# One core, sparse attention and a routed FFN: the output projection's weights loaded in four steps and split head by head, and batch 0's fourth row block in another bank

## The chip, the cores and the metric

One core of a Trainium2 chip runs the whole kernel. The metric is device time in microseconds of one launch, the median of several runs.

## What is computed

The reference, cut to what matters (x is 8 x 512 x 512, H = 16 heads of HD = 128; `attn` mixes compressed, selected and windowed attention with three gates):

```python
z = layernorm(x)
q, k, v = rope(z @ Wq), rope(z @ Wk), z @ Wv      # per head: 512 x 128
o = o_cmp * g_cmp + o_slc * g_slc + o_swa * g_swa # per head and batch
x = x + concat_heads(o) @ Wo                      # Wo: 2048 x 512
x = x + routed_ffn(layernorm(x))                  # top 128 tokens of each batch, capacity 0.125
```

The change touches the place where the first two parts meet: the last heads of the attention, and `concat_heads(o) @ Wo` for batch 0.

## The kernel before, in words

Every product is made of three float32r matmuls, hi*hi, hi*lo and lo*hi, where hi is a rounded copy of an operand and lo is what rounding left out. So each operand needs a "high" (a copy, mostly on ScalarE) and a "low" (a subtraction on GpSimd or VectorE) before TensorE can use it.

**Attention** (`attend`, from line 425) runs over 128 *units*: 8 pairs of heads p, and in each 16 units, numbered u = 16p + 4k + j with k and j from 0 to 3. A unit is one head (s = j % 2) of one batch (b = 2k + j // 2). Every engine has its own program over units, and the order of the work is written out by hand in each; semaphores that count up join them. The stages of a unit are spread over three turns of the loop: in the body of u, TensorE projects q and k of u (L641), scores u - 1 (L684), transposes the probabilities of u - 2 (L698), projects the values of u (L654) and multiplies values with probabilities for u - 2 (L721). ScalarE's body (L804) begins with `output_out` (L783), the copy of a finished output to s_swap, then evacuates q, mixes the far blocks of u - 2 (L793), takes the high part of the values of u - 1 (L801), evacuates k, takes the high parts of the transposed probabilities (`pt_high`, L768), and does the exponentials (L774, L780) and the high parts of q and k (L763). VectorE's body (L928) masks and reduces the scores, takes `pt_low` (L894), forms the coefficients, mixes (L902, L918; the mix of blocks 2 and 1 waits for ScalarE's far mix) and ends with the values' low part (L924). GpSimd (L601) applies the rotary factors and takes the low parts of q and k. SyncE (L520) issues the store of an output (L508) and two swaps (L497, L498: the two halves of a rotated vector exchanged through a DMA), q's first and then k's, which also waits for the store. Unit "128" and "129" are bodies that finish the last two units and project nothing (`body(PAIRS, 0, ...)`).

**The end of attention.** The outputs of all units lie in DRAM. `Chunks` (from line 1050) multiplies them with Wo in four *chunks* of four heads for each batch, k = 0 to 3; `product` (L1103) does the 12 matmuls of each of four row blocks of a chunk into one PSUM bank per row block (`bank`, L1065: banks 4, 5, 7 and 3 for batch 0), which collects over the four chunks. Chunks alternate between two buffers. A chunk's semaphore `chunk_used` rises after its last row block. For batch 0 this is laid into attention's last units by hand:

- SP (L541 to L584): behind the first body of `quad(PAIRS - 1, 2)`, unit 120, all four Wo transfers; behind unit 124 the loads of chunks 0 and 1; the loads of chunks 2 and 3 behind the stores of bodies 129 and 130.
- ScalarE (L844 to L872): `high_wo`, two heads at a time, behind each of units 120 to 127; `high_first(0)`, the high part of chunk 0, behind unit 124; `high_first(1)` after unit 127; `high_first(2)` after body 129 and `high_first(3)` after the last output copy.
- GpSimd (L612 to L634): `low_wo` for heads 0 to 7 behind units 120 to 123, the two halves of chunk 0's low behind units 125 and 126, then chunks 1 to 3.
- VectorE (L988 to L1013): `low_wo` for heads 8 to 15 behind units 124 to 127.
- TensorE (L738 to L748):

```python
        chunks.product(pe, 0, 0, rows=(0,))
        pe.wait_ge(v_lo_done, U)
        body(PAIRS, 0, 0, project=False)
        chunks.product(pe, 0, 0, rows=(1, 2))
        chunks.product(pe, 0, 1, rows=(0, 1, 2))
        body(PAIRS, 0, 1, project=False, score=False, between=lambda: chunks.product(pe, 0, 0, rows=(3,)))
        chunks.product(pe, 0, 1, rows=(3,))
        for k in range(2, chunks.K):
            chunks.product(pe, 0, k)
```

The split buffers of Wo and of the chunks lie in the memory of the transposed inputs, xt_hi and xt_lo, which is why each load waits for a projection of the batch that it overwrites (`projected[2]`).

Of the kernel before, what the change touches and what calls it, by code (L numbers as in the profile page):

```python
# [7 lines left out]
H, HD = 16, 128  # L8
# [388 lines left out]
def attend(nc, phase, banks, m, gates, gates_full, xt_hi, xt_lo, weights, rope_d, misc_d, o_dram, gates_dram, chunks):  # L397
# [95 lines left out]
    def sync(sp):  # L493
# [46 lines left out]

        def quad(p, k, first=False, ahead=False, split=False, wo=False, o=False):  # L541
            body(p, k, 0, gate=first)
            if wo:
                sp.wait_ge(projected[2], unit(p, k, 0))
                for n in range(chunks.K):
                    chunks.load_wo(sp, n)
# [36 lines left out]
        chunks.load_first(sp, 3)  # L583
        sp.wait_ge(out_slot_free, 16 + 16 * U)  # L584

    def gpsimd(pool):
        def turn(u, k):

            pool.wait_ge(evacuated[k], u + 1)
            pool.wait_ge(swapped[k], u * 32 + 32)  # L590
            nc.gpsimd.tensor_tensor(s_full[k][:], s_full[k][:], rope[:, 0, :], ALU.mult).then_inc(cos_done[k], 1)  # L591
            nc.gpsimd.tensor_tensor(s_swap[k][:], s_swap[k][:], rope[:, 1, :], ALU.mult).then_inc(sin_done[k], 1)  # L592
            pool.wait_ge(cos_done[k], u + 1)
            pool.wait_ge(sin_done[k], u + 1)
# [17 lines left out]
        def quad(p, k, split=False, wo=False, o=False):  # L612
# [12 lines left out]
        pool.wait_ge(rope_loaded, 16)  # L625
        for k in range(0, 3):
            quad(0, k)
        for p in range(1, PAIRS):
            quad(p - 1, 3, split=p)
            for k in range(0, 3):  # L630
                quad(p, k, wo=p == PAIRS - 1 and k == 2)
        quad(PAIRS - 1, 3, o=True)
        for k in range(1, chunks.K):
            chunks.low(pool, 0, k)  # L634

    def tensor(pe):
# [21 lines left out]

        def body(p, k, j, project=True, score=True, end=True, between=None):
            u = unit(p, k, j)  # L660
# [41 lines left out]
            if project:  # L702
# [3 lines left out]
                project_values(b, s)  # L706
            if between is not None:
                between()
            if end:
# [4 lines left out]
                for i in range(T):  # L714
# [5 lines left out]
                    for v, x in ((v_hi, pt_hi), (v_hi, pt_lo), (v_lo, pt_hi)):  # L720
                        last = nc.tensor.matmul(banks[6][:, PTQ0[i]:N], v[:, slot, i % 2, :], x[:, PTOFF[i]:PTOFF[i] + w],  # L721
                                                start=(n == 0), stop=(n == 3 * T - 1), skip_group_check=True)
                        n += 1
# [19 lines left out]
        chunks.product(pe, 0, 0, rows=(1, 2))  # L743
        chunks.product(pe, 0, 1, rows=(0, 1, 2))
        body(PAIRS, 0, 1, project=False, score=False, between=lambda: chunks.product(pe, 0, 0, rows=(3,)))
        chunks.product(pe, 0, 1, rows=(3,))
        for k in range(2, chunks.K):
            chunks.product(pe, 0, k)  # L748

    def scalar(act):  # L750
# [32 lines left out]
        def output_out(u):  # L783

            act.wait_ge(out_ready, u - 2)
            act.wait_ge(out_slot_free, (u - 3) * 16 + 16)
            nc.scalar.activation(o_sb[:], banks[6][:, :], ACT.Copy).then_inc(out_evacuated, 1)

# [14 lines left out]

        def body(p, k, j, project=True, score=True, end=True, values=True, output=True, split=False):  # L804
            u = unit(p, k, j)
# [37 lines left out]

        def quad(p, k, split=False, wo=False, o=False):  # L844
# [18 lines left out]
        for p in range(1, PAIRS):  # L863
            quad(p - 1, 3, split=p)
            for k in range(0, 3):
                quad(p, k, wo=0 if p == PAIRS - 1 and k == 2 else False)
        quad(PAIRS - 1, 3, wo=4, o=True)
        body(PAIRS, 0, 0, project=False)
        body(PAIRS, 0, 1, project=False, score=False, values=False)
        chunks.high_first(act, 2)  # L870
        output_out(U + 2)
        chunks.high_first(act, 3)  # L872

    def vector(dve):
# [112 lines left out]

        def quad(p, k, split=False, wo=False):  # L988
            for j in range(4):
                body(p, k, j, split=split if j >= 2 else False)  # L990
                if wo:
                    chunks.low_wo(dve, nc.vector, 4 + j)

# [18 lines left out]
        quad(PAIRS - 1, 3, wo=True)  # L1012
        body(PAIRS, 0, 0, project=False)  # L1013
        body(PAIRS, 0, 1, project=False, score=False)

# [9 lines left out]
class Chunks:  # L1025
# [6 lines left out]
    def __init__(self, nc, at, banks, wo, o_dram):  # L1032
# [28 lines left out]
        self.hi_split, self.lo_split, self.chunk_used = S("hi_split"), S("lo_split"), S("chunk_used")  # L1061
        self.wo_hi_split, self.wo_lo_split = S("wo_hi_split"), S("wo_lo_split")
# [14 lines left out]
    def high_wo(self, act, n):  # L1077
        act.wait_ge(self.wo_loaded[n // 2], 16)
        self.nc.scalar.activation(self.wo_hi[:, 2 * n:2 * n + 2, :], self.wo_raw[:, 2 * n:2 * n + 2, :], ACT.Copy).then_inc(self.wo_hi_split, 1)

    def low_wo(self, eng, ops, n):
        eng.wait_ge(self.wo_hi_split, n + 1)
        ops.tensor_tensor(self.wo_lo[:, 2 * n:2 * n + 2, :], self.wo_raw[:, 2 * n:2 * n + 2, :],
                          f32(self.wo_hi[:, 2 * n:2 * n + 2, :]), ALU.subtract).then_inc(self.wo_lo_split, 1)

# [5 lines left out]

    def low_half(self, pool, k, g, last):
        pool.wait_ge(self.hi_split, k + 1)
        ins = self.nc.gpsimd.tensor_tensor(self.o_lo[k][:, g:g + 2], self.o_raw[k][:, g:g + 2], f32(self.o_hi[k][:, g:g + 2]), ALU.subtract)
        if last:
# [7 lines left out]
    def product(self, pe, b, k, rows=range(T)):  # L1103

        begun = isinstance(b, int) and b == 0
        if rows[0] == 0:
            pe.wait_ge(self.lo_split, b * self.K + k + 1)
            if begun:
                pe.wait_ge(self.wo_lo_split, 2 * k + 2)
        for t in rows:  # L1110
# [648 lines left out]
```

## Time and profile before

| | |
|---|---|
| median of 3 runs | 2390.52 us (2385.95 to 2391.7) |
| the profiled execution, its own time | 2390.49 us |
| its span, first to last instruction | 2388.7 us |
| mean granted TensorE clock | 0.992 |
| TensorE busy | 2313.6 us, 97% |
| VectorE, ScalarE, GpSimd busy | 77%, 62%, 68% |
| the chain that ended last | TensorE 67%, VectorE 11%, GpSimd 9%, ScalarE 5%, DMA 3% |

The span holds, in order, a normalisation of the inputs, attention up to about 1830 us, and the projection, routing and experts after it. The profile names an instruction by the line of the kernel that issues it; a helper's line stands for all its callers, so `L1083` is every low part of Wo. In a timeline a row is start, duration, engine, line, operation and operands, and in square brackets how long the engine was idle before and what released it.

### The profile page before, as it was taken

The page shows a single profiled execution, that of the slowest core. Times are in us where ns is not written, and L with a number is a line of the kernel's source. Part 1 is how long each engine was busy: PE and PEld are TensorE (multiplying, and loading weights), DVE is VectorE, ACT ScalarE, POOL GpSimd, SP SyncE. Part 2 cuts the span into 40 slices and gives each one's busy share as a digit, 9 for nine tenths or more (in the row PEclk, how much of TensorE's full clock was granted, in tenths as well). Part 3 has the DMA queues.
Part 4 walks back from the last instruction along what each step waited for, and adds up shares of the span by engine and source line. Part 5 has one row for each costly group of instructions (what it writes and reads, how often), then busy time and mean ns, then how long its engine had stood idle before and what let it go on. Part 6 is the DMA issues. An engine that isn't in the chain of part 4 may idle for free.

```text
span 2388.7 us, 42080 instructions
## 1 busy us (share of the span) xinstructions
PE 2313.6 (97%) x13200; PEld 2034.8 (85%) x13200; DVE 1836.8 (77%) x6087; ACT 1489.5 (62%) x4165; POOL 1632.8 (68%) x1267
## 2 busy tenths in 40 slices
PE   6999999999999999999999999999998999998998
PEld 5799899989888898999899898989887788886787
DVE  8589898988888898989898888888883665566311
ACT  6577777777777777777777777777773111212343
POOL 2677877787787778777877877787883444444554
PEclk9999999999999999999999999999999999999999
DMA  5222222222222223223222322222333444453332
GB/s 172 74 59 62 73 76 58 72 73 67 54 80 69 61 60 84 65 58 81 67 65 58 87 59 67 63 72 60 124 89 123 162 170 154 152 197 102 109 116 79
DMA packets 143602, 213.34 MB, mean 89 GB/s; under 512 B 15009, under 2 KB 53281, under 8 KB 143393
## 3 DMA queue, kind: packets, MB, share of 16 engines
q1 hardware_dynamic: 137248, 196.17, 27.8%
q10 hardware_dynamic: 4224, 8.39, 0.9%
q0 software_dynamic: 1920, 6.24, 0.8%
q8 instruction: 101, 1.65, 0.3%
q14 instruction: 109, 0.88, 0.1%
HBM read 90.47 MB, written 53.22 MB: 60 GB/s over the span
## 4 chain that ended last, share of the span: by engine, by line
PE 67%; DVE 11%; POOL 9%; ACT 5%; DMA 3%; issue 2%; SPq 0%; POOLq 0%; ACTq 0%; DVEq 0%
PE bank L641 19%; PE bank L1116 13%; PE bank L654 10%; PE bank L684 7%; PE bank L721 7%; PE bank L698 4%; DMA s_swap<-s_full 3%; PE bank L1677 3%; PE bank L1658 3%; POOL s_full L591 2%; POOL s_swap L592 2%; POOL s_full L595 2%; DVE bank L884 1%; DVE shift L880 1%; DVE pt_lo L894 1%
## 5 line engine op out<-in xcount | busy, mean ns | idle before, releaser
L591 POOL TENSOR_TENSOR s_full<-s_full,rope 128x512 f32<-128x512 f32 x256 | 336.5, 1314 | 334.9 <-DMA s_swap<-s_full 334.5
L595 POOL TENSOR_TENSOR s_full<-s_full,s_swap 128x512 f32<-128x512 f32 x256 | 330.7, 1292 | 37.6 <-POOL s_swap L592 0.9
L592 POOL TENSOR_TENSOR s_swap<-s_swap,rope 128x512 f32<-128x512 f32 x256 | 330.7, 1292 | 0.0
L599 POOL TENSOR_TENSOR qk_lo<-s_full,qk_hi 128x512 fp32r<-128x512 f32 x256 | 326.2, 1294 | 0.1
L768 ACT ACTIVATE pt_hi<-bank 128x384 fp32r<-128x384 f32 (+1 forms) x384 | 174.5, 528 | 229.1 <-PE bank L698 229.0
L654 PE MATMUL bank<-wv_hi,xt_hi 128*128 128x256 f32 x1024 | 300.1, 293 | 0.0
L774 ACT ACTIVATE bank<-bank,shift 128x512 f32<-128x512 f32 (+3 forms) x512 | 256.9, 502 | 60.1 <-DVE bank L884 59.8
L1100 POOL TENSOR_TENSOR o_lo<-o_raw,o_hi 128x2048 fp32r<-128x2048 f32 x31 | 142.3, 4591 | 217.6 <-ACT o_hi L1276 185.9
L654 PE MATMUL bank<-wv_hi,xt_lo 128*128 128x256 f32 x1024 | 289.7, 283 | 0.0
L654 PE MATMUL bank<-wv_lo,xt_hi 128*128 128x256 f32 x1024 | 289.7, 283 | 0.0
L884 DVE TENSOR_REDUCE bank<-bank 128x8 f32<-128x512 f32 (+3 forms) x512 | 253.1, 494 | 0.0
L880 DVE TENSOR_REDUCE shift<-bank 128x1 f32<-128x512 f32 (+3 forms) x512 | 246.3, 481 | 0.0
L902 DVE SCALAR_TENSOR_TENSOR bank<-bank,coef,cb 128x192 f32<-128x192 f32 (+1 forms) x512 | 195.5, 405 | 58.6 <-ACT probs L793 58.6
L780 ACT ACTIVATE win<-win,shift 128x192 f32<-128x192 f32 (+1 forms) x512 | 225.8, 441 | 0.0
L763 ACT ACTIVATE qk_hi<-s_full 128x512 fp32r<-128x512 f32 x256 | 161.4, 630 | 93.1 <-POOL s_full L595 89.1
L894 DVE TENSOR_TENSOR pt_lo<-bank,pt_hi 128x384 fp32r<-128x384 f32 (+1 forms) x384 | 206.9, 594 | 8.7 <-ACT pt_hi L768 8.7
L641 PE MATMUL bank<-xt_hi,wq_hi 128*128 128x512 f32 x512 | 207.8, 406 | 0.8 <-PEq L201 0.8
L1116 PE MATMUL bank<-wo_hi,o_hi 128*128 128x512 f32 x512 | 205.9, 402 | 2.1 <-POOL o_lo L1100 2.1
L1116 PE MATMUL bank<-wo_hi,o_lo 128*128 128x512 f32 x512 | 200.6, 392 | 0.0
L641 PE MATMUL bank<-xt_hi,wq_lo 128*128 128x512 f32 x512 | 200.4, 391 | 0.0
L1116 PE MATMUL bank<-wo_lo,o_hi 128*128 128x512 f32 x512 | 200.1, 391 | 0.0
L641 PE MATMUL bank<-xt_hi,wk_lo 128*128 128x512 f32 x512 | 199.2, 389 | 0.0
(189 smaller groups left out, 6899.0 us busy)
## 6 DMA issues: line engine op xcount, KB each, us to landing
s_swap<-s_full SPq DMA_DIRECT2D x512, 128.0 KB, 2.3
o_scratch<-s_swap SPq DMA_DIRECT2D x128, 256.0 KB, 2.0
o_raw<-o_scratch SPq DMA_DIRECT2D x32, 1024.0 KB, 5.4
w_raw<-in_L_ffn_W SPq DMA_DIRECT2D x64, 256.0 KB, 2.9
xin<-in_L_attn_x SPq DMA_DIRECT2D x14, 1024.0 KB, 5.6
z_scratch<-z ACTq DMA_DIRECT2D x8, 1024.0 KB, 4.3
out<-x SPq DMA_DIRECT2D x32, 256.0 KB, 2.1
wq_raw<-in_L_attn_Wq SPq DMA_DIRECT2D x16, 256.0 KB, 3.1
```

Of the source, the lines that this page charges most:

```text
L591: nc.gpsimd.tensor_tensor(s_full[k][:], s_full[k][:], rope[:, 0, :], ALU.mult).then_inc(cos_done[k], 1)
L592: nc.gpsimd.tensor_tensor(s_swap[k][:], s_swap[k][:], rope[:, 1, :], ALU.mult).then_inc(sin_done[k], 1)
L595: nc.gpsimd.tensor_tensor(s_full[k][:], s_full[k][:], s_swap[k][:], ALU.add).then_inc(roped[k], 1)
L599: nc.gpsimd.tensor_tensor(qk_lo[k][:], s_full[k][:], f32(qk_hi[k][:]), ALU.subtract).then_inc(lo_done[k], 1)
L641: last = nc.tensor.matmul(banks[QK_BANK[k]][:, :], w[k][s][:, c, :], v[:, b, c, :], start=(n == 0), stop=(n == 3 * C - 1))
L654: last = nc.tensor.matmul(out, x[:, b, c, at:at + P], w[:, c, :], start=(n == 0), stop=(n == 3 * C - 1), skip_group_check=True)
L774: nc.scalar.activation(n, n, ACT.Exp, bias=shift1[:, t:t + 1], scale=-1.0, accum_out=sums[:, 1, t:t + 1]).then_inc(exp_row, 1)
L780: nc.scalar.activation(win[:, t, lo:], win[:, t, lo:], ACT.Exp, bias=shift2[:, t:t + 1], scale=-1.0, accum_out=sums[:, 2, t:t + 1]).then_i ...
L880: nc.vector.tensor_reduce(shift1[:, t:t + 1], n[:, 0:(t + 1) * P], AX.X, ALU.min)
L884: nc.vector.reduce_sum(sc[:, t, 0:nb], n[:, 0:nb * BS].rearrange("p (n s) -> p n s", s=BS), AX.X).then_inc(row_read, 1)
L894: nc.vector.tensor_tensor(pt_lo[:, PTOFF[g]:PTOFF[g] + w], pt_bank(u, g)[:, 0:w], f32(pt_hi[:, PTOFF[g]:PTOFF[g] + w]), ALU.subtract).then ...
L1116: last = self.nc.tensor.matmul(self.bank(b, t)[:, :], o[k % 2][:, g, t * P:(t + 1) * P], w[:, k * self.G + g, :], start=(k == 0 and n == 0 ...
```

## The change

Wo's transfers are issued one by one, behind units 114, 116, 118 and 120. Wo's high and low parts are made per head (128 x 512) and no longer per two heads: high parts of heads 0 to 9 behind units 116 to 123, 126 and 127, those of 10 to 15 after body 128; low parts of heads 0 to 7 on GpSimd behind units 117 to 124, those of 8 to 15 on VectorE after body 128. Chunk 0's high part is made in two halves behind units 124 and 125, and its low part in four operations; chunk 1's load is issued behind unit 126, its high part made inside body 128 after the values' high part; chunk 2's high part is made inside body 129. The loads of chunks 2 and 3 each move up by one store. Batch 0's fourth row block collects in bank 6, which held the outputs of units; the output of body 129 goes to bank 0 and its transposes to banks 0, 1 and 2. TensorE does row block 3 of chunk 0 and all of chunk 1 before body 129.

```diff
-            return banks[((6, 5, 7), (6, 0, 1))[u - U][g]]
+            return banks[((6, 5, 7), (0, 1, 2))[u - U][g]]
+    def out_bank(u):
+        return banks[0 if isinstance(u, int) and u == U + 1 else 6]
...
+        def load_wo(p, k, j, n):
+            sp.wait_ge(projected[2], unit(p, k, j))
+            chunks.load_wo(sp, n)
+
+        def quad(p, k, first=False, ahead=False, split=False, wo=(), o=False):
             body(p, k, 0, gate=first)
+            if 0 in wo:
+                load_wo(p, k, 0, wo[0])
             if o:
                 sp.wait_ge(projected[2], unit(p, k, 0))
                 chunks.load_first(sp, 0)
-                chunks.load_first(sp, 1)
             body(p, k, 1, ahead=ahead)
             body(p, k, 2, split=split)
+            if 2 in wo:
+                load_wo(p, k, 2, wo[2])
+            if o:
+                chunks.load_first(sp, 1)
             body(p, k, 3, split=split)
...
-        quad(PAIRS - 1, 0, first=True)
-        quad(PAIRS - 1, 1)
-        quad(PAIRS - 1, 2, wo=True)
+        quad(PAIRS - 1, 0, first=True, wo={2: 0})
+        quad(PAIRS - 1, 1, wo={0: 1, 2: 2})
+        quad(PAIRS - 1, 2, wo={0: 3})
         quad(PAIRS - 1, 3, o=True)
         body(PAIRS, 0, 0, project=False, gate=True)
+        chunks.load_first(sp, 2)
         body(PAIRS, 0, 1, project=False)
-        chunks.load_first(sp, 2)
+        chunks.load_first(sp, 3)
         body(PAIRS, 0, 2, project=False)
-        chunks.load_first(sp, 3)
...
@@ gpsimd: quad, and its calls @@
-                if wo:
-                    chunks.low_wo(pool, nc.gpsimd, j)
+                if j in wo:
+                    chunks.low_wo(pool, nc.gpsimd, wo[j], chunks.wo_lo_split)
                 if o and j in (1, 2):
-                    chunks.low_half(pool, 0, 2 * (j - 1), j == 2)
+                    chunks.low_half(pool, 2 * (j - 1), j == 2)
-                quad(p, k, wo=p == PAIRS - 1 and k == 2)
-        quad(PAIRS - 1, 3, o=True)
+                quad(p, k, wo=({}, {1: 0, 2: 1, 3: 2}, {0: 3, 1: 4, 2: 5, 3: 6})[k] if p == PAIRS - 1 else {})
+        quad(PAIRS - 1, 3, wo={0: 7}, o=True)
...
@@ tensor @@
         body(PAIRS, 0, 0, project=False)
         chunks.product(pe, 0, 0, rows=(1, 2))
-        chunks.product(pe, 0, 1, rows=(0, 1, 2))
-        body(PAIRS, 0, 1, project=False, score=False, between=lambda: chunks.product(pe, 0, 0, rows=(3,)))
-        chunks.product(pe, 0, 1, rows=(3,))
+        pe.wait_ge(out_evacuated, U)
+        chunks.product(pe, 0, 0, rows=(3,))
+        chunks.product(pe, 0, 1)
+        body(PAIRS, 0, 1, project=False, score=False)
...
@@ scalar: body (behind values_high and evacuate(u, 1)), quad, and its calls @@
+            if first is not False:
+                chunks.high_first(act, first)
...
-                if wo is not False:
-                    chunks.high_wo(act, wo + j)
-                if o and j == 0:
-                    chunks.high_first(act, 0)
-            if o:
-                act.wait_ge(projected[2], U)
-                chunks.high_first(act, 1)
+                if j in wo:
+                    chunks.high_wo(act, wo[j])
+                if o and j < 2:
+                    chunks.high_half(act, 2 * j)
...
-                quad(p, k, wo=0 if p == PAIRS - 1 and k == 2 else False)
-        quad(PAIRS - 1, 3, wo=4, o=True)
-        body(PAIRS, 0, 0, project=False)
-        body(PAIRS, 0, 1, project=False, score=False, values=False)
-        chunks.high_first(act, 2)
+                quad(p, k, wo=({}, {0: 0, 1: 1, 2: 2, 3: 3}, {0: 4, 1: 5, 2: 6, 3: 7})[k] if p == PAIRS - 1 else {})
+        quad(PAIRS - 1, 3, wo={2: 8, 3: 9}, o=True)
+        body(PAIRS, 0, 0, project=False, first=1)
+        for n in range(10, H):
+            chunks.high_wo(act, n)
+        body(PAIRS, 0, 1, project=False, score=False, values=False, first=2)
         output_out(U + 2)
         chunks.high_first(act, 3)
...
@@ vector @@
-                if wo:
-                    chunks.low_wo(dve, nc.vector, 4 + j)
         body(PAIRS, 0, 0, project=False)
+        for n in range(8, H):
+            chunks.low_wo(dve, nc.vector, n, chunks.wo_late_split)
         body(PAIRS, 0, 1, project=False, score=False)
...
@@ Chunks @@
-        return self.banks[(4, 5, 7, 3)[t] if isinstance(b, int) and b == 0 else t]
+        return self.banks[(4, 5, 7, 6)[t] if isinstance(b, int) and b == 0 else t]
...
+    def high_half(self, act, g):
+        act.wait_ge(self.raw_loaded[0], 16)
+        self.nc.scalar.activation(self.o_hi[0][:, g:g + 2], self.o_raw[0][:, g:g + 2], ACT.Copy).then_inc(self.hi_split if g else self.first_hi_split, 1)
...
+                if k < 2:
+                    pe.wait_ge(self.wo_lo_split, self.G * (k + 1))
+                else:
+                    pe.wait_ge(self.wo_late_split, self.G * (k - 1))
```

## Rows read from the trace of the kernel before

**Rows 1.** The page: TensorE's busy time and share of the span.
```profile
PE 2313.6 (97%) x13200; PEld 2034.8 (85%) x13200; DVE 1836.8 (77%) x6087; ACT 1489.5 (62%) x4165; POOL 1632.8 (68%) x1267
```

**Rows 2.** Windows: length, busy of PE, PEld, DVE, ACT, POOL; clock, DMA.
```profile
1443.32:1549.79 106.47, 106.37 (x659) 96.18 (x658) 94.99 (x340) 78.32 (x239) 80.19 (x64) 1.00 0.24 65
1619.59:1672.85 53.26, 53.26 (x330) 48.05 (x330) 47.20 (x171) 38.44 (x118) 39.30 (x32) 1.00 0.23 60
1672.85:1788.21 115.36, 109.75 (x659) 97.02 (x658) 95.57 (x334) 85.68 (x248) 97.28 (x71) 0.99 0.36 110
1788.21:1830.92 42.71, 32.77 (x155) 27.46 (x154) 22.14 (x75) 19.26 (x52) 14.38 (x7) 0.92 0.19 62
```

**Rows 3.** Windows of single units on TensorE, 122 and 123.
```profile
1700.05:1716.23 16.18, 13.76 (x85) 11.88 (x84) 11.72 (x44) 12.03 (x35) 15.10 (x12) 1.00 0.19 50
1716.23:1729.76 13.53, 13.50 (x84) 11.93 (x84) 11.68 (x44) 10.60 (x32) 12.29 (x10) 1.00 0.23 60
```

**Rows 4.** The tile wo_raw: times in ns and starts; DMA landing.
```profile
L1083 POOL TENSOR_TENSOR wo_lo<-wo_raw,wo_hi x4: 2364/2388/2397, 1691.1 to 1734.5; 128x1024 fp32r<-128x1024 f32 x4
L1083 DVE TENSOR_TENSOR wo_lo<-wo_raw,wo_hi x4: 1215/1216/2362, 1752.8 to 1798.2; 128x1024 fp32r<-128x1024 f32 x4
DMA to landing us min/median/max: 6.0/9.1/11.3
```

**Rows 5.** Timeline of SP's queue, units 121, 124 and 125.
```profile
1691.24 0.47 SPq L497 DMA_DIRECT2D s_swap<-s_full  x1
...
1695.88 0.46 SPq L497 DMA_DIRECT2D s_swap<-s_full  x1
...
1738.01 1.19 SPq L1075 DMA_DIRECT2D o_raw<-o_scratch  x2
...
1750.03 0.47 SPq L497 DMA_DIRECT2D s_swap<-s_full  x1
...
1752.23 0.46 SPq L497 DMA_DIRECT2D s_swap<-s_full  x1
```

**Rows 6.** Timeline of VectorE: far-mix waits, a v_lo, a pt_lo.
```profile
1664.20 0.75 DVE L902 SCALAR_TENSOR_TENSOR bank<-bank,coef,cb 128x192 f32<-128x192 f32 x2 [0.24 <-ACT probs L793]
...
1665.51 0.68 DVE L924 TENSOR_TENSOR v_lo<-bank,v_hi 128x512 fp32r<-128x512 f32 x1
...
1721.85 0.75 DVE L902 SCALAR_TENSOR_TENSOR bank<-bank,coef,cb 128x192 f32<-128x192 f32 x2 [0.93 <-ACT probs L793]
...
1796.30 0.75 DVE L902 SCALAR_TENSOR_TENSOR bank<-bank,coef,cb 128x192 f32<-128x192 f32 x2 [2.24 <-ACT probs L793]
...
1821.48 1.62 DVE L894 TENSOR_TENSOR pt_lo<-bank,pt_hi 128x512 fp32r<-128x512 f32 x3 [7.57 <-ACT pt_hi L768]
```

**Rows 7.** Timeline of ScalarE at the end of attention.
```profile
1792.04 1.05 ACT L1079 ACTIVATE wo_hi<-wo_raw 128x1024 fp32r<-128x1024 f32 x1
1792.99 1.90 ACT L1090 ACTIVATE o_hi<-o_raw 128x2048 fp32r<-128x2048 f32 x1
...
1794.79 0.59 ACT L787 ACTIVATE s_swap<-bank 128x512 f32<-128x512 f32 x1
...
1810.08 0.59 ACT L787 ACTIVATE s_swap<-bank 128x512 f32<-128x512 f32 x1
```

**Rows 8.** Timeline of TensorE from unit 128 to chunk 2.
```profile
1798.34 0.48 PE L684 MATMUL bank<-qk_hi,qk_hi 128*128 128x128 f32 x1 [7.17 <-DVE v_lo L924]
...
1806.55 0.44 PE L1116 MATMUL bank<-wo_hi,o_hi 128*128 128x512 f32 x1
...
1820.22 1.25 PE L698 MATMUL bank<-misc,probs 128*128 128x128 f32 x10
...
1830.92 0.50 PE L1116 MATMUL bank<-wo_hi,o_hi 128*128 128x512 f32 x1 [2.06 <-POOL o_lo L1100]
```

**Rows 9.** A window in unit 128's scores, columns as in rows 2.
```profile
1800.00:1802.00 2.00, 2.00 (x8) 1.90 (x7) 1.90 (x7) 0.00 (x0) 0.00 (x0) 0.50 0.00 0
```

**Rows 10.** Timeline of GpSimd: the low part of chunk 1.
```profile
1794.97 4.52 POOL L1100 TENSOR_TENSOR o_lo<-o_raw,o_hi 128x2048 fp32r<-128x2048 f32 x1 [1.30 <-ACT o_hi L1090]
```

More of the change, by code:

```diff
@@ L539, in body @@
                 weights.load_v(sp, ahead)
-        def quad(p, k, first=False, ahead=False, split=False, wo=False, o=False):
+        def load_wo(p, k, j, n):
+            sp.wait_ge(projected[2], unit(p, k, j))
+            chunks.load_wo(sp, n)
+        def quad(p, k, first=False, ahead=False, split=False, wo=(), o=False):
             body(p, k, 0, gate=first)
-            if wo:
-                sp.wait_ge(projected[2], unit(p, k, 0))
-                for n in range(chunks.K):
-                    chunks.load_wo(sp, n)
+            if 0 in wo:
+                load_wo(p, k, 0, wo[0])
             if o:
@@ L610, in body, with quad @@
                 weights.low(pool, nc.gpsimd, split, 1, j % 2)
-        def quad(p, k, split=False, wo=False, o=False):
+        def quad(p, k, split=False, wo=(), o=False):
             for j in range(4):
                 body(p, k, j, split if j >= 2 else False)
-                if wo:
-                    chunks.low_wo(pool, nc.gpsimd, j)
+                if j in wo:
+                    chunks.low_wo(pool, nc.gpsimd, wo[j], chunks.wo_lo_split)
                 if o and j in (1, 2):
-                    chunks.low_half(pool, 0, 2 * (j - 1), j == 2)
+                    chunks.low_half(pool, 2 * (j - 1), j == 2)
         nc.gpsimd.memset(shift2[:], 0.0).then_inc(out_slot_free, 16)
@@ L657, in project_values, with body @@
             last.then_inc(projected[2], 1)
-        def body(p, k, j, project=True, score=True, end=True, between=None):
+        def body(p, k, j, project=True, score=True, end=True):
             u = unit(p, k, j)
@@ L706, in body @@
                 project_values(b, s)
-            if between is not None:
-                between()
             if end:
@@ L720, in body @@
                     for v, x in ((v_hi, pt_hi), (v_hi, pt_lo), (v_lo, pt_hi)):
-                        last = nc.tensor.matmul(banks[6][:, PTQ0[i]:N], v[:, slot, i % 2, :], x[:, PTOFF[i]:PTOFF[i] + w],
+                        last = nc.tensor.matmul(out_bank(u)[:, PTQ0[i]:N], v[:, slot, i % 2, :], x[:, PTOFF[i]:PTOFF[i] + w],
                                                 start=(n == 0), stop=(n == 3 * T - 1), skip_group_check=True)
@@ L786, in output_out @@
             act.wait_ge(out_slot_free, (u - 3) * 16 + 16)
-            nc.scalar.activation(o_sb[:], banks[6][:, :], ACT.Copy).then_inc(out_evacuated, 1)
+            nc.scalar.activation(o_sb[:], out_bank(u - 1)[:, :], ACT.Copy).then_inc(out_evacuated, 1)
         def mix_far(v, t):
@@ L802, in values_high, with body @@
                                  banks[7][:, :].rearrange("p (a n) -> p a n", a=2), ACT.Copy).then_inc(v_hi_done, 1)
-        def body(p, k, j, project=True, score=True, end=True, values=True, output=True, split=False):
+        def body(p, k, j, project=True, score=True, end=True, values=True, output=True, split=False, first=False):
             u = unit(p, k, j)
@@ L842, in body, with quad @@
                 weights.high(act, split, 1, j % 2)
-        def quad(p, k, split=False, wo=False, o=False):
+        def quad(p, k, split=False, wo=(), o=False):
             for j in range(4):
                 body(p, k, j, split=split if j >= 2 else False)
-                if wo is not False:
-                    chunks.high_wo(act, wo + j)
-                if o and j == 0:
-                    chunks.high_first(act, 0)
-            if o:
-                act.wait_ge(projected[2], U)
-                chunks.high_first(act, 1)
+                if j in wo:
+                    chunks.high_wo(act, wo[j])
+                if o and j < 2:
+                    chunks.high_half(act, 2 * j)
         nc.scalar.activation(gates_full[:], gates_full[:], ACT.Sigmoid).then_inc(gates_squashed, 1)
@@ L986, in body, with quad @@
                 weights.low(dve, nc.vector, split, 0, j % 2)
-        def quad(p, k, split=False, wo=False):
+        def quad(p, k, split=False):
             for j in range(4):
                 body(p, k, j, split=split if j >= 2 else False)
-                if wo:
-                    chunks.low_wo(dve, nc.vector, 4 + j)
         nc.vector.memset(sc, 0.0).then_inc(zeros_set, 3)
@@ L1077, in high_wo, with low_wo @@
     def high_wo(self, act, n):
-        act.wait_ge(self.wo_loaded[n // 2], 16)
-        self.nc.scalar.activation(self.wo_hi[:, 2 * n:2 * n + 2, :], self.wo_raw[:, 2 * n:2 * n + 2, :], ACT.Copy).then_inc(self.wo_hi_split, 1)
-    def low_wo(self, eng, ops, n):
+        act.wait_ge(self.wo_loaded[n // self.G], 16)
+        self.nc.scalar.activation(self.wo_hi[:, n, :], self.wo_raw[:, n, :], ACT.Copy).then_inc(self.wo_hi_split, 1)
+    def low_wo(self, eng, ops, n, split):
         eng.wait_ge(self.wo_hi_split, n + 1)
-        ops.tensor_tensor(self.wo_lo[:, 2 * n:2 * n + 2, :], self.wo_raw[:, 2 * n:2 * n + 2, :],
-                          f32(self.wo_hi[:, 2 * n:2 * n + 2, :]), ALU.subtract).then_inc(self.wo_lo_split, 1)
+        ops.tensor_tensor(self.wo_lo[:, n, :], self.wo_raw[:, n, :], f32(self.wo_hi[:, n, :]), ALU.subtract).then_inc(split, 1)
+    def high_half(self, act, g):
+        act.wait_ge(self.raw_loaded[0], 16)
+        self.nc.scalar.activation(self.o_hi[0][:, g:g + 2], self.o_raw[0][:, g:g + 2], ACT.Copy).then_inc(self.hi_split if g else self.first_hi_split, 1)
     def high_first(self, act, k):
@@ L1090, in high_first, with low_half @@
         self.nc.scalar.activation(self.o_hi[k % 2][:], self.o_raw[k % 2][:], ACT.Copy).then_inc(self.hi_split, 1)
-    def low_half(self, pool, k, g, last):
-        pool.wait_ge(self.hi_split, k + 1)
-        ins = self.nc.gpsimd.tensor_tensor(self.o_lo[k][:, g:g + 2], self.o_raw[k][:, g:g + 2], f32(self.o_hi[k][:, g:g + 2]), ALU.subtract)
+    def low_half(self, pool, g, last):
+        pool.wait_ge(self.hi_split if g else self.first_hi_split, 1)
+        for i in range(g, g + 2):
+            ins = self.nc.gpsimd.tensor_tensor(self.o_lo[0][:, i], self.o_raw[0][:, i], f32(self.o_hi[0][:, i]), ALU.subtract)
         if last:
```

6 lines of the change are left out of this document (3 added, 3 removed).

## The prediction

> **What bounds the kernel now.** I read the page first: TensorE (PE) is busy 97% of a span of 2388.7 us [rows 1]. A change can gain only where PE idles, runs at the lower clock, or is held to another engine's pace. So I read stretches of PE's work next [rows 2]. Undisturbed, eight units (one head of one batch each) take 106.47 us, 13.31 each. Units 116 to 119 take 53.26, the same pace. The last eight, 120 to 127, take 115.36: 8.9 us too long. From the last unit's end, 1788.21 (called S below), to the first product of chunk 2, 1830.92, pass 42.71 us with PE busy 32.77. Those two stretches are all that the diff touches.
>
> Inside the slow eight most units take about 13.53, as unit 123 does, and unit 122 takes 16.18 [rows 3]. Three causes can be read off. First, the four Wo transfers are issued together and take 6.0 to 11.3 us to land [rows 4]; the swap traffic behind them ran into them: unit 121's two swaps are issued 4.64 us apart, where 2.20 is usual (unit 125's) [rows 5]. Second, ScalarE (ACT) splits a Wo part between a unit's last high part and the output copy; behind that copy stand the far mixes that VectorE (DVE) waits for. That wait is 0.24 us without Wo work, 0.93 with it, and 2.24 in the last unit, where the split of chunk 1 stands there too [rows 6]. Third, DVE has its own Wo part, 1.22 us, in units 124 to 127 [rows 4].
>
> At the end PE does row 0 of chunk 0, then idles 7.17 us for the last v_lo, and starts unit 128 at 1798.34 = S+10.13. After it come five product rows, then unit 129 with one row on either side of its values, and a 2.06 us wait for chunk 2's low part [rows 8].
>
> **Units 116 to 127.** ACT's eight Wo splits of 128x1024 become sixteen of one head: ten in units 116 to 123, 126 and 127, six after unit 128. The 128x1024 one costs ACT 0.95 us from start to start, the 128x2048 one 1.80 [rows 7]; on that line one of 128x512 costs 0.52. Units 121 and 123 carried 0.95 of it and took 13.53; taking back 0.43 gives 13.1, under PE's own 13.31, so these units are PE's again. Units 124 and 125 carry half of chunk 0 each, 128x1024, as unit 123 carried a Wo part: 13.55.
>
> POOL's eight heads in units 117 to 124 cost half of 2.39 us each [rows 4], in its waiting for swaps: with a whole 2.39 it was busy 12.29 of unit 123's 13.53 us [rows 3]. The two halves of chunk 0's low (two operations each now, the same columns) lie there in units 125 and 126. If that cover went, each would delay the next unit's scores by up to 1.2 us.
>
> SP issues the four Wo transfers singly, behind the second swap of units 114, 116, 118 and 120, and chunk 1's load behind 126's. Each is some 10 us ahead of the next store; issuing one costs SP 0.5 us, with nothing due. The two 1 MB loads at 1738.01 stood in the same place, and the next pair of swaps left 2.20 us apart, 12 us later [rows 5]. So I take no cost; the bounds are 0 and 2.9 us a load, the excess of unit 122 behind the burst of four.
>
> Sum: ten units at 13.37 (13.31 and a little for the fuller ACT) and two at 13.55 are 160.8 us, against 53.26 + 115.36 = 168.6. Gain **7.8 us**. Bounds: 9.0 (all at 13.3) and 5.9 (all at 13.56).
>
> **From S to chunk 2.** Before the last v_lo ACT has one head (0.52) instead of a Wo part and chunk 1 (2.75 [rows 7]): 2.2 us less, and DVE's wait of 2.24 [rows 6] shrinks to little. DVE's own Wo work in the four units is gone as well, so it no longer lags PE. In a steady unit v_lo ended at 1666.19, 6.6 us after PE began that unit (1659.60, one steady 13.25 before unit 120). I take S+7.0, where it was S+10.1. Gain **3.1**, bounds 2.4 and 3.5. Next after it comes POOL's low part of k at S+5.5, not later.
>
> Unit 128 itself is 8.2 us up to 1806.55 (T) [rows 8]; about 2.5 of it is the granted clock of 0.50, the 1.2 GHz level, after the idle time [rows 9]. I keep that: PE still idles 4 us. Chunk 1's high split (1.8 us) moves inside this unit on ACT, ahead of pt_high; what hides it is PE's scores and transposes, 3.7 us or more. POOL's low of chunk 1 follows it and must be there for PE at T+10; it is 9 us early.
>
> The work from T to chunk 2 stays 22.3 us (24.37 less the wait of 2.06), but its order brings two waits. **Row 3 of chunk 0** now uses bank 6, so PE stands before it until ACT has copied out unit 128's output (out_evacuated of U). ACT reached that copy at 1810.08, T+3.5; now the six left-over heads are in front of it: 6 x 0.52 = 3.1, plus 0.59 for the copy: T+7.3. PE is through rows 1 and 2 after 24 products of 0.228 (60 of them took 13.67 [rows 8]), T+5.5. Cost **1.8**, bounds 1.5 and 2.5, and all of PE's queue stands behind it. **Unit 129** has no product row between its transposes and its values any more. DVE's first pt_lo began 1.26 after the transposes did [rows 6, 8] and lasts about 0.6; PE is done with them at +1.0. Cost **1.0**, bounds 0.7 and 1.5.
>
> The wait of 2.06 goes: chunk 2's split needs chunk 0 used, now near T+10, then 1.9 on ACT and 4.5 on POOL, and PE comes for it at T+25. Its load and chunk 3's move up by one store on SP; chunk 3's waits there for chunk 1's low, long done. Chunk 3 has the whole of chunk 2, 10.9 us, for its own 6.5.
>
> The eight heads that DVE splits after unit 128 start when the far mixes, behind ACT's six heads, are done: about T+10. Eight at half of 1.22 end at T+15; PE asks for DVE's next pt_lo near T+22. Nothing.
>
> POOL can take from that cover. The one DVE Wo part that began (1798.2) while POOL worked on chunk 1's low took 2.36 us, not 1.22 [rows 4], ending 1.07 after POOL's did [rows 10]: it waited for it. The same beside chunk 2's low, from T+12 to T+16.7, puts the eight heads at T+20: 2 us are left.
>
> The Trainium skill, page "SBUF — State Buffer", section "Who interferes with whom", says that GpSimd and a VectorE operation with two SBUF inputs lock each other out for a whole instruction. By that rule the trace agrees.
>
> **Sum.** 7.8 + 3.1 + 2.06 - 1.8 - 1.0 = 10.2 us. After chunk 2 each step waits for steps that moved along with it, so the gain stays. The profiled execution took 2390.49 us, 1.8 around its span; the median of three is 2390.52, so the sum holds for both: 2380.3. A measurement of this kernel can tell about 0.3%, 7.2 us, from no change.
>
> **Rivals.**
> 1. ACT sets the pace in all twelve units, 13.56 each: they give 5.9 and the total is 8.3 us, 2382.2. For it: DVE waits for ACT's far mixes even without Wo work, 0.24 us. Against: there it did not lengthen the unit. Chance 0.17.
> 2. The end is tighter than I count: the wait before row 3 drops the clock again, 1.5 us as a part of what it cost in unit 128, and the DVE heads are 2 us late for pt_lo, with a second hold by POOL. Then 10.2 - 3.5 = 6.7 or a little less: near 2384. Against: 2 us of slack, and 5.5 us of dense products before the wait. Chance 0.13.
> 3. Slower: each single Wo load delays the next store and swaps as the burst did, 2.9 us at four places, 11.6 in all; 10.2 becomes -1.4: 2391.9. It decides where a load still runs 10 us after its issue. The burst's first landed in 6.0 [rows 4], so one alone would have to be much slower than one of four. Chance 0.06.
> 4. It doesn't do what it says: the slow units owe their time to something that stays. Then only the end gains, 2 to 5 us: 2387. Against: the waits on ACT and the swaps name Wo work each time. Chance 0.07.
>
> The forecast has 0.57. Its own range, from the bounds (9.0 + 3.5 + 2.1 - 1.5 - 0.7 = 12.4; 6.5 + 2.4 + 2.1 - 2.5 - 1.5 = 7.0), is 2378 to 2383.5. The range of 8 in 10 takes in the second rival and something of the spread of the runs (2385.95 to 2391.7): 2375.5 to 2386.5. Faster by more than 0.3% (below 2383.3) holds the forecast, most of rival 1 and a third of rival 2: 0.74. Within 0.3%: 0.22. Slower: 0.04.
>
> **What would show it.** Units 121 to 127 of 13.3 to 13.6 us, none of 16; swaps never over 2.5 us apart; PE's idle time before unit 128 near 4 us; a new PE wait for ACT's copy before row 3 of chunk 0, 1.5 to 2; about 1 us before unit 129's values; none before chunk 2; 40.3 us from S to chunk 2. I am wrong if the twelve units take over 163 us, if POOL or a swap shows as PE's releaser in them, or if the time from S to chunk 2 is not under 42.7.

## The result and the profile after

The changed kernel takes 2376.74 us (median of 6 runs, 2373.81 to 2379.06) against 2390.72 for the kernel before; the ratio is 0.9939, 95% interval 0.9929 to 0.9949. That is 14 us less (12.2 to 17.0), where 10.2 were forecast. A second, separate set gave 0.9932 (0.9919 to 0.9945). The forecast's own range was 2378 to 2383.5 and its wide one 2375.5 to 2386.5: the measured time lies 1.3 us under the first and inside the second. One of the 12 executions of a kernel below, the one with the end's order alone, ran in a slow state (2985.89 us at a granted clock of 0.72) and is left out of its ratio.

The first view is that of rows 2 and 3: windows of the changed kernel's profiled execution (span 2377.1 us). In order: units 116 to 119, units 120 to 127, unit 122 alone, and the last unit's end to chunk 2. Columns as in rows 2.

```profile
1619.18:1672.99 53.81, 53.49 (x330) 48.00 (x330) 46.94 (x169) 39.07 (x120) 41.47 (x34) 1.00 0.35 99
1672.99:1781.31 108.32, 107.56 (x658) 95.76 (x658) 93.38 (x336) 83.50 (x252) 94.69 (x76) 1.00 0.30 88
1700.75:1714.02 13.27, 13.27 (x84) 12.00 (x84) 11.76 (x44) 10.33 (x33) 11.58 (x10) 1.00 0.23 61
1781.31:1820.69 39.38, 32.23 (x155) 26.71 (x154) 23.53 (x76) 20.49 (x55) 15.45 (x6) 0.96 0.21 68
```

Units 116 to 119 take half a microsecond more (53.26 before), units 120 to 127 give 7.0 (115.36), unit 122 alone 2.9 (16.18 [rows 3]), and the end gives 3.3 (42.71).

More than unit 122's 2.9 comes from a unit whose length neither the rows nor the forecast give. Unit 125 of the kernel before (first line) took 16.94 us, the longest of the eight, and takes 13.63 in the changed one (second line):

```profile
1743.49:1760.43 16.94, 15.10 (x84) 13.53 (x84) 13.29 (x48) 12.97 (x35) 11.66 (x9) 0.90 0.28 87
1740.54:1754.17 13.63, 13.51 (x85) 11.94 (x84) 11.38 (x42) 10.45 (x30) 11.50 (x10) 1.00 0.22 60
```

What it waited for before, on ScalarE, VectorE and TensorE:

```profile
1746.18 1.05 ACT L1079 ACTIVATE wo_hi<-wo_raw 128x1024 fp32r<-128x1024 f32 x1
1747.13 1.91 ACT L1090 ACTIVATE o_hi<-o_raw 128x2048 fp32r<-128x2048 f32 x1
1748.93 0.59 ACT L787 ACTIVATE s_swap<-bank 128x512 f32<-128x512 f32 x1
...
1750.92 0.75 DVE L902 SCALAR_TENSOR_TENSOR bank<-bank,coef,cb 128x192 f32<-128x192 f32 x2 [2.73 <-ACT probs L793]
...
1752.04 0.69 PE L684 MATMUL bank<-qk_hi,qk_hi 128*128 128x384 f32 x1 [1.84 <-DVE probs L918]
```

A Wo part and the whole high part of chunk 0 stood before ScalarE's output copy, 2.75 us, as chunk 1's did in the last unit. The change puts half a chunk there instead, and no Wo head: VectorE's wait is 1.33 us and TensorE's is gone.

Next SP's queue around unit 121, to set beside rows 5, and the landing of the Wo transfers from the tile's view.

```profile
1681.81 0.60 SPq L1079 DMA_DIRECT2D wo_raw<-in_L_attn_Wo  x1
1691.45 0.34 SPq L512 DMA_DIRECT2D o_scratch<-s_swap  x1
1691.94 0.47 SPq L501 DMA_DIRECT2D s_swap<-s_full  x1
...
1694.13 0.46 SPq L501 DMA_DIRECT2D s_swap<-s_full  x1
...
DMA to landing us min/median/max: 5.4/6.4/7.1
```

The last single Wo transfer leaves 9.6 us before the next store and has landed by then (7.1 us at most), and the two swaps of unit 121 are 2.19 us apart and no longer 4.64.

TensorE from the end of the units to chunk 2, as in rows 8:

```profile
1788.09 0.47 PE L693 MATMUL bank<-qk_hi,qk_hi 128*128 128x128 f32 x1 [3.81 <-DVE v_lo L932]
...
1793.67 0.47 PE L728 MATMUL bank<-pt_hi,v_hi 128*128 128x512 f32 x1 [0.85 <-ACT pt_hi L776]
...
1802.91 0.50 PE L1132 MATMUL bank<-wo_hi,o_hi 128*128 128x512 f32 x1 [1.63 <-ACT s_swap L795]
...
1818.75 0.47 PE L728 MATMUL bank<-pt_hi,v_hi 128*128 128x512 f32 x1 [0.85 <-ACT pt_hi L776]
```

The idle time before unit 128 has gone from 7.17 to 3.81 us and the 2.06 before chunk 2 are gone. Two waits are new: 1.63 for ScalarE's copy before row 3 of chunk 0, and 0.85 before unit 129's values.

### The profile page after: what moved, and what is told of

It is laid out like the page before. It is cut to its first block, busy times and chain, and to the rows that moved or that the text cites. A ratio compares the mean times of both kernels' runs of the same rounds, so it can differ in the third digit from the quotient of the medians.

```text
span 2377.1 us, 42098 instructions
## 1 busy us (share of the span) xinstructions
PE 2309.4 (97%) x13200; PEld 2031.2 (85%) x13200; DVE 1844.1 (78%) x6091; ACT 1489.1 (63%) x4174; POOL 1633.4 (69%) x1273
## 4 chain that ended last, share of the span: by engine, by line
PE 66%; DVE 11%; POOL 9%; ACT 5%; DMA 3%; issue 2%; SPq 0%; POOLq 0%; ACTq 0%; DVEq 0%
PE bank L650 19%; PE bank L1132 13%; PE bank L663 10%; PE bank L693 7%; PE bank L728 7%; PE bank L707 4%; DMA s_swap<-s_full 3%; PE bank L1693 3%; PE bank L1674 3%; POOL s_full L600 3%; POOL s_swap L601 3%; POOL s_full L604 3%; DVE bank L892 1%; DVE pt_lo L902 1%; DVE shift L888 1%
## 5 line engine op out<-in xcount | busy, mean ns | idle before, releaser
L650 PE MATMUL bank<-xt_hi,wk_hi 128*128 128x512 f32 x512 | 199.2, 389 | 0.0
```

Of the source, the lines that this page charges most:

```text
L650: last = nc.tensor.matmul(banks[QK_BANK[k]][:, :], w[k][s][:, c, :], v[:, b, c, :], start=(n == 0), stop=(n == 3 * C - 1))
```

## The experiments

**The end's order alone, and all but the end's order.** The first kernel is the one before with the change's banks and TensorE order; the second is the changed one with those of before:

```diff
...
-        chunks.product(pe, 0, 1, rows=(0, 1, 2))
-        body(PAIRS, 0, 1, project=False, score=False, between=lambda: chunks.product(pe, 0, 0, rows=(3,)))
-        chunks.product(pe, 0, 1, rows=(3,))
+        pe.wait_ge(out_evacuated, U)
+        chunks.product(pe, 0, 0, rows=(3,))
+        chunks.product(pe, 0, 1)
+        body(PAIRS, 0, 1, project=False, score=False)
...
```

> The kernel before with the end's order of the change alone: bank 6 for the fourth row block, TensorE's row 3 of chunk 0 and all of chunk 1 ahead of unit 129, the loads of chunks 2 and 3 one store earlier, chunk 2's high part inside body 129. The Wo work over the units stays. Theory A (the order itself gains little, its new waits eat the 2.06 us wait that goes): without the six heads in front of ScalarE's output copy no wait before row 3, about 0.9 us before unit 129's values, none before chunk 2: the time from unit 128's end to chunk 2 goes from 24.4 to 23.2 us, total -1.2 us (-0.05%). Theory B (the order is where the gain that I did not forecast lies): -4 us or more.

> The changed kernel with the end's order of before: banks 3 and 6 as before, five product rows and then unit 129, chunk 2's load and high part as before. Theory A (the gain is the Wo work over the units and the earlier v_lo): from 1619 to the last unit's end 162 us as in the changed kernel, 24.4 us from unit 128's end to chunk 2 instead of its 25.1, so the same as or 0.7 us under the changed kernel, -12 to -15 us against before. Theory B (the order carries it): only -8 to -10 us.

The order alone: 2389.53 us, ratio 0.9992 (0.9983 to 1.0000). From unit 128's end to chunk 2 it took 1830.37 - 1807.21 = 23.16 us, 1.2 less than before, as theory A had it. All but the order: 2374.88 us, ratio 0.9938 (0.9925 to 0.9950), not to be told from the changed kernel; by the medians it is 15.5 us under the kernel before, half a microsecond more than theory A's 12 to 15. Its units 116 to 127 took 160.22 us, and its old order ends in the old wait:

```profile
1817.21 0.50 PE L1134 MATMUL bank<-wo_hi,o_hi 128*128 128x512 f32 x1 [2.06 <-POOL o_lo L1115]
```

That is 24.40 us from unit 128's end (1792.81), against 25.10 in the changed kernel. With the six heads in front of the output copy the new order costs 0.7 us; only without them is it a gain.

**Only the Wo transfers, and only VectorE's Wo parts.** The first issues the four transfers singly as the change does. The second moves `low_wo` on VectorE:

```diff
-        quad(PAIRS - 1, 3, wo=True)
+        quad(PAIRS - 1, 3)
         body(PAIRS, 0, 0, project=False)
+        for n in range(4, 8):
+            chunks.low_wo(dve, nc.vector, n)
```

> The kernel before with the four Wo transfers issued singly behind units 114, 116, 118 and 120, all else unchanged. Theory A (the burst cost unit 122 its 2.9 us, and a single load costs nothing): unit 122 goes from 16.18 to about 13.5 us, no other unit longer, total -2.7 us (-0.11%). Rival (a single load costs as well, or unit 122 is long for another reason): 0 or slower, with late swaps in units 115, 117, 119 or 121.

> The kernel before with VectorE's four Wo parts (1.22 us each) moved behind its body of unit 128, all else unchanged. Theory A (they set the pace of units 125 to 127): those go from 13.3, 14.7 us and the lag before the last v_lo to 13.5 each, PE's idle time before unit 128 from 7.17 to about 5.5 us (ScalarE's 2.75 us before the copy stay), total -3 to -4 us. Rival (ScalarE's splits alone hold these units): under 1 us.

Single transfers: 2386.72 us, ratio 0.9989 (0.9980 to 0.9997). Unit 122 took 13.65 us, 2.5 less, units 115 to 119 13.26 each, unit 120 13.99: theory A. Unit 125 still took 16.92 us. (A slip stands at unit 120 in nearly every kernel, 13.3 to 14.3 us, with Wo loads near it or without.) VectorE's parts moved: 2387.5 us, ratio 0.9991 (0.9982 to 0.9999). From unit 123 to unit 128's scores it took 1796.20 - 1717.62 = 78.58 us, against 82.11 before and 81.45 in the second profile of the kernel before, below: 3.5 and 2.9 less, near theory A's 3 to 4, with 6.20 us of idle time left before unit 128. But units 125 to 127 took 15.43, 13.54 and 13.69 us, not 13.5 each. In unit 125 TensorE still waited, 1.90 us, so VectorE's part was not what held it there:

```profile
1744.38:1759.81 15.43, 13.53 (x84) 11.96 (x84) 11.72 (x44) 12.48 (x33) 10.25 (x9) 1.00 0.31 94
```

That unit took 16.9 to 17.1 us in four profiles, at a clock of 0.90, and 15.4 in two, at 1.00; TensorE's wait was 1.84 to 1.94 in all six. With the Wo transfers and VectorE's parts each ruled out by a run, ScalarE's 2.75 us remain, which the waits name; no run moved them alone.

One thing here I had not looked for. The kernel with VectorE's parts moved still has the burst, and its unit 122 took 19.11 us; that of the kernel with the order alone took 18.06.

**The same two kernels again.**

> The changed kernel as it is, for a second profile and a tighter ratio. Theory A (I sized the removed burst by one profile in which unit 122 took 16.18 us, while two others with the burst showed 18.06 and 19.11): units 121 to 124 within 13.3 to 13.6 us each again, 161 to 163 us for units 116 to 127, 39 to 40 us from the last unit's end to chunk 2, and -13 to -14 us against before. Rival (the extra gain lies in something of the changed kernel's that its first profile did not show): a stretch over 1 us shorter than in that profile.

> The kernel before as it is, for a second profile. Theory A (the burst of Wo transfers costs a varying amount, 2.9 us in the first profile and 4.8 and 5.9 in two other kernels that kept it): unit 122 between 16 and 19.5 us, the stall of 3.5 to 4 us at GpSimd's indirect DMA in the experts present again, PE's idle time before unit 128 7.17 us. Rival (18 and 19 us came from those kernels' own edits): unit 122 at 16.2 again.

The windows of the changed kernel again: units 116 to 127, then to chunk 2, then to the end. Behind them those of the kernel before again, with unit 122 third.

```profile
1618.73:1778.86 160.13, 159.86 (x987) 144.07 (x986) 140.76 (x504) 123.14 (x370) 136.10 (x109) 1.00 0.32 93
1778.86:1818.41 39.55, 32.33 (x154) 26.83 (x154) 23.52 (x76) 20.56 (x55) 15.51 (x6) 0.96 0.20 67
1818.41:2373.40 554.99, 532.18 (x2354) 433.87 (x2353) 267.65 (x567) 146.74 (x186) 253.60 (x150) 0.99 0.42 142
```

```profile
1619.44:1790.59 171.15, 163.97 (x986) 146.21 (x986) 143.18 (x502) 124.75 (x364) 136.77 (x102) 0.98 0.31 93
1790.59:1832.83 42.24, 32.18 (x155) 26.86 (x154) 22.11 (x75) 19.29 (x52) 14.32 (x7) 0.92 0.19 63
1699.65:1719.25 19.60, 16.45 (x85) 14.57 (x84) 13.13 (x50) 13.63 (x43) 18.21 (x15) 0.83 0.15 41
1832.83:2390.50 557.67, 533.26 (x2352) 434.74 (x2352) 259.40 (x565) 146.24 (x185) 253.00 (x150) 0.99 0.41 141
```

The burst's price varies, and the first profile had it at its cheapest: unit 122 took 16.18, 18.06, 19.11, 17.63 and 19.60 us in the five profiles that have the burst, 18.1 on the mean, so 4.8 over 13.3 instead of 2.9. The clock column (third from the right) goes with it: 1.00 in the first [rows 3], 0.91, 0.82, 0.90 and 0.83 in the others, so for a part of the unit the granted clock was at its lower level, 1.2 GHz. The length of the wait alone does not decide that: TensorE's wait for GpSimd's low part before the unit's scores was 1.64 us in the first and 2.66, 1.74, 1.71 and 2.35 in the others. Theory A for the changed kernel missed two numbers: its units took 160.1 us, below 161 to 163, and by the ratio it gained 16.3 us, above 13 to 14. By its wording the rival holds as well, since the units were 2.0 us shorter than in the first profile and the stretch after chunk 2 1.4. In the kernel before again, unit 122 was 0.1 above the forecast's 19.5.

**After chunk 2.** The last windows above show 2.7 us that the change gains where it touches nothing. The first pair of profiles has 557.8 and 556.4 us there. TensorE's rows with idle time differ by more than half a microsecond in one place, in the experts. GpSimd and TensorE in the kernel before:

```profile
2243.38 0.18 POOL L1583 CAST row_at<-away 128x1 int32<-128x1 f32 x1
2247.09 1.11 POOL L1588 DMA_INDIRECT rows<-out,row_at  x1 [3.53 <-issue]
```

```profile
2249.55 0.50 PE L1658 MATMUL bank<-zsel_hi,w_hi 128*128 128x512 f32 x1 [1.82 <-POOL w_lo L1576]
```

And GpSimd at the same place in the changed kernel:

```profile
2234.80 0.18 POOL L1599 CAST row_at<-away 128x1 int32<-128x1 f32 x1
2235.82 1.11 POOL L1604 DMA_INDIRECT rows<-out,row_at  x1 [0.84 <-POOL row_at L1599]
```

GpSimd stood 3.5 us with nothing to wait for ("issue"), the next weight's low part came late, and TensorE waited 1.82 us. So I made GpSimd's program six instructions longer, and nothing else:

```diff
-        nc.gpsimd.memset(mc[:], 0.0).then_inc(chunks.chunk_used, 1)
+        for t in range(T - 1):
+            nc.gpsimd.memset(mc[:, t:t + 1], 0.0)
+        nc.gpsimd.memset(mc[:, T - 1:T], 0.0).then_inc(chunks.chunk_used, 1)
...
```

> The kernel before with three memsets on GpSimd, at the start of attention, split into nine: the same values, six more instructions in GpSimd's program, as many as the change adds there, and no other edit. Theory A (in the experts, 420 us after attention, GpSimd stands 3.5 to 4.0 us at one indirect DMA with nothing to wait for, in all four kernels with the old GpSimd program and in none of the six with the longer one; the place of the instructions in memory decides): the stall at that DMA goes or moves, TensorE's wait of 1.8 to 2.3 us for w_lo behind it goes with it, total -1.8 us (-0.08%). Rival (the stall has to do with the Wo work or the end's order): it stays at 3.5 us or more at the same line, total 0.

2386.25 us, ratio 0.9983 (0.9974 to 0.9992), and the same DMA has its usual wait:

```profile
2243.25 1.11 POOL L1593 DMA_INDIRECT rows<-out,row_at  x1 [0.84 <-POOL row_at L1588]
```

The stall stood in all five profiles with the old GpSimd program and in none of the seven with a longer one, and six more memsets, 2170 us earlier, take it away.

The 4.1 us between the medians (1.9 to 6.2 by the interval) are more than the 1.8 that I expected, because the wait is not the whole price. The matmuls behind it, 2249.55 to 2254.23, ran at a granted clock of 0.64. From the matmul behind an earlier wait of 0.9 us to the span's end it took, before and with the longer program (columns as in rows 2):

```profile
2239.25:2388.70 149.45, 140.12 (x604) 113.99 (x604) 24.93 (x34) 60.50 (x99) 83.81 (x81) 0.97 0.35 108
2238.10:2384.60 146.50, 138.60 (x604) 112.86 (x604) 32.91 (x34) 60.39 (x98) 84.10 (x81) 0.99 0.35 110
```

It was 149.45 to 149.95 us in the five profiles with the stall and 146.42 to 146.52 in the seven without: the stall costs 3.3 us on the means. What lies between chunk 2 and there took 405.0 to 410.0 us in the twelve profiles, whether they have the stall or not, so the 2.7 and 1.4 us of the two pairs are the stall's price with this scatter on top.

That six instructions more in the program decide is shown, for this one length. That the stall is the loading of code is not, but the DMA view points there. In the window of the stall, 2243.56 to 2247.09, the queue marked "instruction" has one packet (count, MB, share):

```profile
q14 instruction: 1, 0.01, 0.7%
```

The same holds for the stall in each of the five profiles. In the seven others that queue has no packet in the 3.5 us before the same DMA. Whose instructions they are the profile doesn't say.

**Toward a better kernel.** Three edits to the changed one: ScalarE's six heads behind the output copy; TensorE's wait for the last v_lo moved to the first transposes that write its bank; a product row in front of unit 129's values.

```diff
-        for n in range(10, H):
-            chunks.high_wo(act, n)
-        body(PAIRS, 0, 1, project=False, score=False, values=False, first=2)
+        body(PAIRS, 0, 1, project=False, score=False, values=False, first=2, heads=range(10, H))
...
-        pe.wait_ge(v_lo_done, U)
         body(PAIRS, 0, 0, project=False)
...
+                    if not project and g == 2:
+                        pe.wait_ge(v_lo_done, U)
...
-        chunks.product(pe, 0, 1)
-        body(PAIRS, 0, 1, project=False, score=False)
+        chunks.product(pe, 0, 1, rows=(0, 1, 2))
+        body(PAIRS, 0, 1, project=False, score=False, between=lambda: chunks.product(pe, 0, 1, rows=(3,)))
```

> The changed kernel with ScalarE's six left-over Wo heads moved behind the output copy and the far mixes of body 129. Theory A (they alone are what TensorE waits for before row 3 of chunk 0): the wait of 1.63 us goes to 0, 0.85 before unit 129's values stays, from unit 128's end to chunk 2 23.5 us instead of 25.1; total -1.6 us against the changed kernel, so about -15.5 against before. Rival (the copy is late for the exponentials before it): a wait of over 0.5 us stays.

> The changed kernel with TensorE's wait for the last v_lo moved from before unit 128 to before its third group of transposes, the first that writes v_lo's bank. Theory A (the idle time before unit 128 is that wait, and next come the low parts of q and k, ready near S+4.7): scores start at S+4.7 instead of S+6.8, PE's idle time 3.8 us goes to about 1.7, and the granted clock stays at 1.00, so that the scores take 2.1 us and not 3.5: -2 to -3.4 us against the changed kernel. Rival (the scores wait for the mixed probabilities of unit 126 instead, which come from the same far mixes): -0.5 us or less.

> The changed kernel with both edits, and with row 3 of chunk 1 between unit 129's transposes and its values, to cover the 0.85 us there. Theory A: the three add up: no wait before row 3, none before unit 129's values, 22.6 us from unit 128's end to chunk 2, unit 128 2 to 3.4 us earlier; -4.5 to -6 us against the changed kernel, near 2371.5 us. Rival (each hides behind the other): -3 or less.

Copy first: 2373.69 us, ratio to before 0.9925 (0.9912 to 0.9938). The wait before row 3 is gone, and from unit 128's end to chunk 2 pass 1816.92 - 1793.75 = 23.17 us, 1.9 less than the changed kernel's 25.10: theory A. By the medians of this set it is 1.4 us under the changed kernel (2375.14), too little to tell them apart by time alone; the same goes for the next kernel.

Wait behind the scores: 2373.62 us, ratio 0.9921 (0.9909 to 0.9933). TensorE starts unit 128 at 4.70 us after the last unit's end (1782.28), as expected. The windows of its scores show the miss: the clock did not stay up (third column from the right of the windows).

```profile
1786.98 0.30 PE L693 MATMUL bank<-qk_hi,qk_hi 128*128 128x128 f32 x1 [1.74 <-POOL qk_lo L608]
```

```profile
1787.00:1789.00 2.00, 2.00 (x9) 1.65 (x10) 1.99 (x6) 2.00 (x3) 0.00 (x0) 0.73 0.74 206
1789.00:1791.00 2.00, 2.00 (x11) 2.00 (x10) 1.87 (x6) 0.57 (x2) 1.37 (x1) 0.50 1.02 376
```

Even 1.74 us of idle time there was followed by the half clock, the 1.2 GHz level, so unit 128 ended 2.2 us earlier and not up to 3.4. (In unit 125 of the kernel before again, 1.85 us were not: the unit's clock was 1.00.)

All three: **2370.42 us**, ratio to before 0.9906 (0.9892 to 0.9919); the changed kernel in the same set had 0.9932. The end takes 1813.28 - 1779.30 = 33.98 us instead of 39.55, with no wait from unit 128's values on. The three add up, 4.7 us less than the changed kernel by the medians and 5.6 in the profiles.

## Why the prediction was right, and what it missed

The waits that it named went and the two that it added came, in the sizes that it gave. Its account of the slow units had a hole, though, and a gain came after chunk 2, where it saw none: without the stall's 3.3 us the 14 measured would be some 10.7, beside the 10.2 forecast.

- *The units.* Forecast 160.8 us for 116 to 127; the two profiles show 162.13 and 160.13, and the four other kernels with this schedule 160.2, 160.4, 160.4 and 161.7. The first profile's extra lies in units 117 (14.04) and 120 (14.30), with short waits for VectorE's probabilities. Units 125 to 127, paced by the halves and the last heads, took 13.63, 13.58 and 13.56 in the first. Rival 1 (13.56 in all twelve, 162.7) is neared by the first alone, and not for its reason: units 122 to 124 took 13.27 there. Rival 3 is out: a single transfer lands in 5.4 to 7.1 us, under the 10 that it had. So is rival 4: units 122, 125 and 127 are slow no more. The swaps kept to 2.5 us apart but for one pair in unit 116, 2.7.
- *"Inside the slow eight most units take about 13.53."* That reading was wrong. The eight took 13.66, 13.54, 16.18, 13.53, 13.73, 16.94, 13.26 and 14.52 us, and the largest excess, in unit 125, stood in no row. The sum came out all the same, because it subtracts from the measured 168.6 us as a whole, and because the change halves chunk 0's high part, which, by the waits, is what unit 125 stood for. That part of the 7.8 was right by luck.
- *The burst, the term that was mis-sized.* The 168.6 us hold unit 122's excess of 2.9 us, from the one profile. It is 4.8 on the mean of five, and the units gain 8.8 on the mean of two profiles each (169.9 to 161.1), not 7.8.
- *The range.* Its low end adds 6.5 for the units where the bound worked out above it is 5.9: 6.4 in all, not 7.0.
- *From S to chunk 2.* Forecast 3.1 + 2.06 - 1.8 - 1.0 = 2.4 us; measured 3.3, and 3.0 on the mean of two pairs. v_lo came at S+6.8 (7.0). The new waits were 1.63 (1.8) and 0.85 (1.0), and 25.10 us lay between unit 128's end and chunk 2, where 25.1 was forecast. Unit 128 was 0.7 shorter (7.5 us for 8.2): I kept its low clock whole, and the clock over the stretch was 0.96 and not 0.92. The shorter idle time does not explain it: the unit took 8.2 us behind 3.99 us of idle time (copy first) and 7.7 behind 7.15 (the kernel before again). What decides stays open. Rival 2 did not come: behind the wait of 1.63 us the products were 0.23 us apart again from the second on, and VectorE's heads were done at T+14.4.
- *"After chunk 2 each step waits for steps that moved along with it, so the gain stays."* This step failed. A GpSimd stall of 3.5 to 4 us in the experts hung on the length of GpSimd's program, which the change makes longer, and with it went 3.3 us of TensorE's time: a wait of 1.8 to 2.3 us and the lower clock behind it. I had priced each added GpSimd instruction at its duration and never as program.
- *VectorE's heads and the lock.* They cost nothing, as forecast, but the other engine waited. I had VectorE held behind chunk 2's low, up to T+20. Its heads ran through in 4.90 us and GpSimd stood:

```profile
1805.08 4.90 DVE L1092 TENSOR_TENSOR wo_lo<-wo_raw,wo_hi 128x512 fp32r<-128x512 f32 x8
```

```profile
1808.02 6.43 POOL L1113 TENSOR_TENSOR o_lo<-o_raw,o_hi 128x2048 fp32r<-128x2048 f32 x1 [14.79 <-ACT o_hi L1102]
```

GpSimd's operation of 4.5 us took 6.43 and ended 4.47 after VectorE's last head (1809.98). The Trainium skill, page "SBUF — State Buffer", section "SBUF: two separate sides", gives the pair of ports to whichever operation starts first. The trace agrees, and shows in addition that back-to-back heads did not let GpSimd in between; the second profile of the changed kernel has the same 4.90 and 6.43 us.

On the means of the pairs the parts are 8.8, 3.0 and 2.0 after chunk 2: 13.8 us, near the 14 that was measured. The 2.0 are the stall's 3.3 less 1.2 us by which the stretch ahead of it happened to be longer in the changed kernel's two profiles.

## What to carry to other kernels

A wait's price read from one profile is a sample; where transfers collide, look at a second execution before sizing it. List the length of every unit in a slow stretch before explaining it by one: the longest here was not looked at. Wide work in the gap between the last high part and the copy that frees others is paid by all of them, so put the copy first: moving six copies behind it took 1.9 us out of the end, the new bank order alone 1.2. When a kernel has a long unrolled program on an engine, look for idle time put down to "issue": here six instructions added 2170 us earlier took it off the critical path.

## What the runs showed that I had not expected

- A stall of 3.5 to 4.0 us on GpSimd, present or absent by six instructions elsewhere in its program; 3.3 us of TensorE's time, 0.14% of the whole.
- The same burst of four 1 MB transfers cost unit 122 between 2.9 and 6.3 us in five profiles. Its landing hardly tells: 6.0 to 11.3 us both where the unit took 16.18 and where it took 17.63.
- The clock fell to its lower level in unit 128 after 1.74 us of idle time, following a dense row of products. In unit 125 waits of 1.84 to 1.94 us were followed by the lower level in four profiles and not in two, for 1.5 us of difference.
